# A four-layer graph network on one core: ScalarE instead of VectorE makes the row one-hots of blocks 3 and 7 in the counting stage

## The reference

```
s1 = Wh @ a1;  s2 = Wh @ a2
e = leaky_relu(s1[src] + s2[dst])     # maximum over all edges is needed
h' = sum over edges of softmax(e) * Wh[...]
nbr_sum = segment_sum(x[src], dst)    # layer 1
```

## Time and profile before

| | us |
|---|---|
| median of 3 runs (lowest, highest) | 8727.64 (8727.42, 8731.45) |
| the profiled execution, its own time | 8728.76 |
| its span, first to last instruction | 8726.9 |
| busy in the span: PE, PEld, DVE, ACT, POOL | 7226.3, 5596.3, 6060.3, 5246.3, 3328.1 |
| counting stage, from about 113 to 1757 us of the span | 1644 |

### The profile page before, as it was taken

The page is one execution under the profiler, slowest core; times in us unless marked ns, Lnnn a source line. Parts: engine busy times, 40 slices in busy tenths (PEclk is TensorE's granted clock), DMA queues, the critical chain, the costliest instruction groups (busy, mean ns, idle before and its releaser), DMA issues. The chain is left out here.

```text
span 8726.9 us, 195704 instructions
## 1 busy us (share of the span) xinstructions
PE 7226.3 (83%) x51013; PEld 5596.3 (64%) x51014; DVE 6060.3 (69%) x12581; ACT 5246.3 (60%) x9329; POOL 3328.1 (38%) x3274
## 2 busy tenths in 40 slices
PE   5999999978859999999777777777778888887775
PEld 3665666667758888888555555556556666666554
DVE  7988988989983333333666666666667777777777
ACT  3666666678856666666444444444457777776553
POOL 0000000000000000000577777777747777777776
PEclk8999999999989999999888888888889999999896
DMA  3333333366644444442222222222236666666665
GB/s 110 140 134 136 138 137 137 138 213 224 226 136 133 133 133 133 132 133 92 66 54 54 54 54 54 54 54 54 54 115 206 207 208 203 207 207 197 195 196 157
DMA packets 629186, 1179.06 MB, mean 135 GB/s; under 512 B 215307, under 2 KB 289340, under 8 KB 609685
## 3 DMA queue, kind: packets, MB, share of 16 engines
q1 hardware_dynamic: 499834, 860.28, 30.4%
q0 software_dynamic: 129280, 317.93, 13.0%
HBM read 901.19 MB, written 276.57 MB: 135 GB/s over the span
## 5 line engine op out<-in xcount | busy, mean ns | idle before, releaser
L2270 POOL DMA_INDIRECT att_kv_rows<-kv_dram,att_stage x1616 | 1624.8, 1005 | 594.8 <-issue 487.5
L2025 POOL DMA_INDIRECT conv_rows<-y_dram,conv_stage x1616 | 1635.8, 1012 | 501.0 <-issue 479.6
L1014 DVE SCALAR_TENSOR_TENSOR mean_rest<-mean_counts,mean_high 128x896 f16<-128x896 f32 x343 | 376.9, 1099 | 858.0 <-ACT mean_high L975 857.9
L695 PE MATMUL conv_part<-conv_msgs,conv_hot 128*128 128x256 f32 x3232 | 950.1, 447 | 0.0
L2003 ACT ACTIVATE conv_hid<-conv_hid_ps 100x512 f32<-100x512 f32 x408 | 221.4, 594 | 1187.3 <-PE conv_hid_ps L2034 1187.3
L695 PEld LDWEIGHTS conv_part<-conv_msgs,conv_hot 128*128 128x128 f32 x3232 | 715.7, 233 | 109.7
L1068 PE MATMUL mean_sum_ps<-wh,mean_turned 128*128 128x129 f32 x4802 | 693.4, 284 | 62.5 <-ACT mean_turned L983 62.2
L235 PE MATMUL count_ps<-count_cols,count_rows 128*128 128x392 bf16 x3920 | 729.0, 331 | 10.0 <-DVE count_cols L201 10.0
L519 PE MATMUL soft_ps<-wh,soft_weights 128*128 (+1 forms) x4802 | 580.1, 280 | 142.5 <-DVE soft_weights L463 142.5
L201 DVE TENSOR_SCALAR count_cols<-cols,col_key 128x784 bf16<-128x784 f16 x1960 | 686.2, 417 | 0.0
L2034 PE MATMUL conv_hid_ps<-conv_scalars,conv_w 10*100 10x512 f32 x816 | 280.8, 764 | 480.9 <-DMA conv_scalars<-in_scalars 479.8
(11 more groups left out here) (279 smaller groups left out, 16420.4 us busy)
## 6 DMA issues: line engine op xcount, KB each, us to landing
c_dram<-count_counts SPq DMA_DIRECT2D x392, 392.0 KB, 2.3
mean_counts<-c_dram SPq DMA_DIRECT2D x343, 448.0 KB, 3.6
att_w_rows<-w_dram SPq DMA_DIRECT2D x404, 256.0 KB
soft_counts<-c_dram SPq DMA_DIRECT2D x98, 1024.0 KB, 4.9
w_dram<-mlp_w SPq DMA_DIRECT2D x245, 256.0 KB, 2.6
soft_counts<-c_dram SPq DMA_DIRECT2D x49, 1088.0 KB, 5.0
att_lanes<-lo_dram SPq DMA_DIRECT2D x404, 128.0 KB
mlp_feats<-in_feats SPq DMA_DIRECT2D x246, 192.0 KB, 2.7
```

The source lines that it names most:

```text
L695: ins = nc.tensor.matmul(part, c.hot[:, s, t, :], rows[:, t, :], start=half == 0 and t == 0, stop=half == 1 and t == T - 1)
L1014: nc.vector.scalar_tensor_tensor(rest[:, m], counts[:, m], 0.25, high[:, m], ALU.mult, ALU.subtract).then_inc(rest_done, 1)
L2025: pool.indirect_dma_start(rows[:, s, t, :], None, y_dram, bass.IndirectOffsetOnAxis(ap=stage[:, s, t:t + 1], axis=0)).then_inc(gathered[s] ...
L2270: pool.indirect_dma_start(kv_rows[:, s, t, :], None, kv_dram, bass.IndirectOffsetOnAxis(ap=stage[:, s, t:t + 1], axis=0)).then_inc(gathere ...
```

## The change

Blocks v = 3 and v = 7 of each iteration no longer have their row one-hots made by VectorE. ScalarE makes them, one block ahead: at v = 2 and at v = 6, before its MLP activations and before `count_take` of that v, it runs `count_rows(v + 1)`. That is five Squares of (row_key - lane) into a new f32 buffer, then one Relu of 1 - square into the bf16 buffer, which is 1 where the two are equal and 0 elsewhere. TensorE waits for it at those two blocks, and VectorE waits for the squares before it moves the lane numbers.

```diff
+COUNT_BY_SCALAR = (3, 7)
...
+        self.gap_rows = sb("gap_rows", [P, T0, P])
...
+        self.rows_squared = sem("count_rows_squared")
+        self.rows_done = sem("count_rows_done")
...
     dve.wait_ge(c.counted, k + 1)
     if v == 0:
         dve.wait_ge(c.lanes_moved, i + 1)
-    nc.vector.tensor_tensor(c.rows[:, b], at.lanes[:, v].unsqueeze(1).to_broadcast([P, T0, P]),
-                            over(at.row_key[:, bass.ds(first, T0)], [P, T0, P], 2), ALU.is_equal)
+    if v not in COUNT_BY_SCALAR:
+        nc.vector.tensor_tensor(c.rows[:, b], at.lanes[:, v].unsqueeze(1).to_broadcast([P, T0, P]),
+                                over(at.row_key[:, bass.ds(first, T0)], [P, T0, P], 2), ALU.is_equal)
...
+def count_rows(nc, act, c, at, i, v):
+
+    k, b = VB * i + v, v % 2
+    n = len(COUNT_BY_SCALAR) * i + COUNT_BY_SCALAR.index(v)
+    word = act.value_load(at.words[:, bass.ds(k, 1)], min_val=0, max_val=2 ** 31 - 1)
+    first = nc.s_assert_within(act.snap(word & 2047), 0, NT - T0, skip_runtime_bounds_check_because="windows begin at tiles")
+
+    act.wait_ge(c.lanes_moved, i + 1)
+    for t in range(T0):
+        ins = nc.scalar.activation(c.gap_rows[:, t], at.lanes[:, v], ACT.Square, scale=-1.0, bias=at.row_key[:, bass.ds(first + t, 1)])
+    ins.then_inc(c.rows_squared, 1)
+
+    act.wait_ge(c.counted, k + 1)
+    act.wait_ge(c.rows_squared, n + 1)
+    nc.scalar.activation(c.rows[:, b], c.gap_rows[:], ACT.Relu, scale=-1.0, bias=1.0).then_inc(c.rows_done, 1)
...
     pe.wait_ge(c.gap_done, k + 1)
     pe.wait_ge(c.hot_done, k + 1)
+    if v in COUNT_BY_SCALAR:
+        pe.wait_ge(c.rows_done, len(COUNT_BY_SCALAR) * i + COUNT_BY_SCALAR.index(v) + 1)
...
                     for v in range(VB):
+                        if v + 1 in COUNT_BY_SCALAR:
+                            count_rows(nc, act, c, at, i, v + 1)
                         if v in COUNT_PAIR0:
                             mlp.scalar(nc, act, UB * i + COUNT_PAIR0[v], range(2))
...
                             dve.wait_ge(c.hot_done, VB * i + v + 1)
                             dve.wait_ge(c.free_x, 1)
+                            dve.wait_ge(c.rows_squared, len(COUNT_BY_SCALAR) * (i + 1))
                             nc.vector.tensor_scalar(at.lanes[:], at.lanes[:], float(VB * P), None, ALU.add).then_inc(c.lanes_moved, 1)
```

## The result

| | before | changed |
|---|---|---|
| median of 4 runs (us) | 8729.55 | 8914.41 |
| lowest, highest | 8727.42, 8732.55 | 8909.98, 8919.03 |
| ratio, 95% interval | | 1.0212 (1.0194 to 1.0229) |

What follows compares the result with a forecast made beforehand. TensorE was taken to set the counting stage's pace, meeting only ScalarE late. 49 x 2.24 = 109.8 us on the profiled 8728.8 us gave 8838.6, which lies 1.1 us above the median: 8837 us (+1.3%), range 8805 to 8905.

Steps and rivals of the forecast that it cites:

- Where the time goes: Counting stage: the call at v = 6 delays TensorE's second layer of u2 by 2.24 us; v = 2 costs 0.
- The price of the call: ScalarE, counting stage: five Squares and a Relu of 640 columns take 2.24 us a call, 4.48 us an iteration.
- The register read: ScalarE, before a call's first Square: a word read into a register, taken as covered, 0; uncovered 0.82 us.
- The added waits of VectorE: VectorE waits for the squares at v = 7; what follows comes up to 0.4 us later, cost 0.
- VectorE's relief: Counting stage: one 128x640 comparison fewer in two of eight blocks, worth 0 to 10 us, taken as 0.
- One sign: Sign to look for: VectorE's busy time down by 72 us or more.
- The table: ScalarE, counting stage: Square and Silu share a table, so table loads stay at x49.
- rival (b): ScalarE, counting stage: Square and Silu don't share a table, loads of 1.283 us add up to 294 us, 9022; chance 0.04.
- The clock: TensorE after the new stall at v = 6: whether the clock falls; the forecast sum of 109.8 us has no such term.
- Rival (a): TensorE's clock falls at the new stall at v = 6: 1.37 us each, 67 us more, 8904; chance 0.08.
- the likeliest case: Whole kernel: 49 stalls of 2.24 us at v = 6, 8837 us, spanning 8805 to 8877; chance 0.77.
- The upper end of the range: Whole kernel: 8905 us, set to take in the case where the clock falls at the new stall, 8904.

Runs made afterwards that it cites:

- Block 7 alone: The changed kernel with ScalarE making the rows of block 7 only, block 3 back on VectorE: 8895.48 us, ratio 1.0202.
- block 3 alone: The changed kernel with ScalarE making the rows of block 3 only, block 7 back on VectorE: 8720.79 us, ratio 1.0000.
- both calls hidden: The changed kernel with block 7's Squares moved to v = 5 and its Relu behind the Silus of v = 6: 8720.87 us, ratio 1.0000.
- the last experiment: One Silu ahead of the counting loop: on the kernel before, 8671.48 us; on the kernel with block 7's Squares at v = 5, 8672.22 us.

## Why the prediction was right and where it failed

- **Where the time goes: right.** One place, the call at v = 6, one new wait at the second layer of u2, in TensorE's in-order stream, not given back later. Block 7 alone gave 176 us, block 3 alone nothing.
- **The price of the call: nearly right.** 2.24 us was worked out, 2.39 measured (827.40 to 829.79). Squares at 395 ns and the Relu at 737 ns came as forecast. The difference is the step from the Squares to the Relu: 0.18 us of idle time at v = 6, where the earlier trace rows have 0.03. Block 7 alone has 2.29 (856.70 to 858.99) and a stall of 2.33. The register read was covered, as assumed; uncovered, the Squares would have come 0.8 us late, but they start 0.79 us after the start of the Relu before them (826.61 to 827.40), the usual distance without idle time.
- **The added waits of VectorE: right.** It waits 1.05 us for the squares and no one waits for it in turn: TensorE's waits for its one-hots are 8.2 us in the stage, for 10.0 before.
- **VectorE's relief: right at 0, to within 8 us.** 8720.87 against 8719.05 with both calls hidden. One sign was off: its busy time was to fall by 72 us or more, and over the whole kernel it fell by 59 (6060.3 to 6001.5).
- **The table: right.** x49 before and after; rival (b) is out. The single load of the earlier trace rows was the row that told it, and the last experiment shows the reason for the 49: entering the loop with the table in place leaves one.
- **The clock: the step that failed.** Rival (a) had the mechanism, its place and its sum, 8904 us, with a chance of 0.08. The text against it was: "2.3 is shorter than both, and one of the two was harmless." From one harmless and one harmful stall above 3 us it inferred that a shorter one would be mostly harmless; two events don't bear that. In fact 44 of 49 stalls of 2.4 us were harmful, and the stall of 3.17 us in the earlier trace rows was the exception: 2 of 49 at 3.03 us were harmless, and the two long waits for the column one-hots, 3.14 to 3.27 us, stand in all twelve traces, where 20 of the 24 are followed by slow products (2.31 us or more instead of 1.82). The size was low as well: 1.37 us came from ten products of 128x392; the 32 products that stand behind this stall lose 1.62. With 117.0 + 71 the sum comes out; with the term left at 0 in the likeliest case it does not. The upper end of the range, 8905, was (a) with the call at 2.24 us and no margin of its own; the call was 0.15 us dearer and the slower products cost 71 us instead of 67, and so the time fell 9 us outside.

## What to carry to other kernels

Work moved to an engine with idle time is free only if it lands in that idle time: look at the timeline for what stands right behind the new instructions and who waits for it, and put them ahead of an instruction that waits anyway. Where TensorE gets a new regular stall, price the products behind it at the lower clock too, by a row where they ran so, and give that case its chance by more than one or two stalls of the trace; in this kernel 1.5 us cost nothing more, 2.0 us cost it in 4 cases of 10 and 2.4 us in 9 of 10. A load of ScalarE's table that recurs in a loop may go away if its function is used once ahead of the loop.

## What had not been expected of the hardware

The fall of the clock is not a matter of yes or no at one length of stall. With the same loop around it, its share rose, one profiled execution each, from 0 of 49 at 1.54 us over 21, 38 and 44 of 49 at 2.02, 2.33 and 2.42 us to 47 of 49 at 3.03 us. In the middle of that range the cost is steep: 0.48 us of stall, from 1.54 to 2.02, raised the loss by 67.5 us, of which 49 x 0.48 = 24 are the stall and the rest slower products. And useless products that keep TensorE going pay here in time: 13 of them in each stall won back some 60 us.
